# Banded attention on one core: the value's low half taken from a float32 copy by GpSimd, and three buffers of probability halves

## What is computed

```python
x = x + broadcast(v[:, 1:2]),  v = layernorm(x) @ W.T + b      # one row per sequence
x = x + ffn(layernorm(x))                                       # two mixes, sigmoid gate
# attention, 16 heads of 64, seen as rows of 1024-long sequences; banded, window 128
q, k = rope(proj(Wq, bq)), rope(proj(Wk, bk)); v = proj(Wv, bv)
scores = (q_block @ concat(k_previous_block, k_block).T) / 8, masked to kj in [qi, qi + 128]
ctx = softmax(scores) @ concat(v_previous_block, v_block)
x = x + ctx @ Wo.T + bo
x = x + ffn(layernorm(x))
```

## Time and profile before

| | |
|---|---|
| median of three runs | 1597.86 us |
| the profiled execution | 1600.48 us, its span 1598.6 us |
| busy over the span: TensorE, VectorE, ScalarE, GpSimd | 94%, 88%, 83%, 71% |
| TensorE granted clock, mean over the span | 0.985 |
| busy of 400 us in the middle of the attention: TensorE, VectorE, ScalarE, GpSimd | 382.25, 372.32, 338.95, 325.26 us |
| TensorE, line 1693 | 256 products with minus the identity |
| ScalarE, line 1530 | 128 copies of the low half |

### The profile page before, as it was taken

One profiled execution on the slowest core, in us unless ns is written; L12 is line 12 of the kernel. 1 busy time (PEld: TensorE's weight loads), 2 busy tenths in 40 slices (PEclk: granted clock), 3 DMA queues, 4 the chain that ended last, 5 costly groups with the idle time before them and its releaser, 6 DMA issues. The chain is left out here.

```text
span 1598.6 us, 46975 instructions
## 1 busy us (share of the span) xinstructions
PE 1497.0 (94%) x16866; PEld 1144.6 (72%) x16866; DVE 1403.0 (88%) x3860; ACT 1323.6 (83%) x2442; POOL 1134.8 (71%) x909
## 2 busy tenths in 40 slices
PE   5999978899999999999999999999999999889998
PEld 4888745577777677766767776766677777678887
DVE  6999669999999999999999999999999999857885
ACT  5999668888888888888888888888888878759996
POOL 4665367778787887877787878787887777623443
PEclk8999999999999999999999999999999999989999
DMA  5242248899999999999999999999999998962331
GB/s 214 93 126 93 90 80 140 166 173 174 181 176 175 170 172 174 182 172 179 171 173 172 168 180 178 177 173 179 168 168 169 177 162 159 174 162 85 107 107 67
DMA packets 729886, 247.94 MB, mean 155 GB/s; under 512 B 689588, under 2 KB 716472, under 8 KB 729656
## 3 DMA queue, kind: packets, MB, share of 16 engines
q1 hardware_dynamic: 711816, 228.93, 75.6%
q10 hardware_dynamic: 17840, 16.00, 3.7%
HBM read 47.73 MB, written 25.17 MB: 46 GB/s over the span
## 5 line engine op out<-in xcount | busy, mean ns | idle before, releaser
L1502 ACT ACTIVATE at_prob<-at_prob,at_top 128x256 f32<-128x256 f32 (+1 forms) x1024 | 428.3, 491 | 20.0 <-DVE at_top L1338 17.7
L1338 DVE CUSTOM_DVE_ANT_0 at_prob<-banks,at_masks,pre_s_scale 128x256 f32<-128x256 f32 (+1 forms) x1024 | 421.0, 471 | 26.5 <-PE banks L1778 10.1
L1350 DVE TENSOR_TENSOR at_halves<-at_prob,at_halves 128x1024 f16<-128x1024 f32 (+1 forms) x256 | 333.1, 1301 | 4.4 <-ACT at_halves L1511 4.3
L1663 PE MATMUL banks<-at_xt,pre_w_h 128*128 128x512 f16 x1024 | 298.2, 384 | 7.5 <-ACT at_v_l L1530 4.7
L1778 PE MATMUL banks<-at_kt,at_qt 32*128 32x256 f32 (+1 forms) x4096 | 252.4, 382 | 45.1 <-POOL at_qt L1240 20.5
L1778 PEld LDWEIGHTS banks<-at_kt,at_qt 32*128 32x128 f32 x4096 | 197.7, 186 | 106.7 <-issue 102.1
L1511 ACT ACTIVATE at_halves<-at_prob 128x1024 f16<-128x1024 f32 (+1 forms) x256 | 263.4, 1029 | 6.1
L1734 PE MATMUL banks<-at_v_h,at_pt 128*128 128x65 f16 x1984 | 208.7, 195 | 11.6 <-DMA at_pt<-at_halves 7.6
L1220 POOL TENSOR_TENSOR at_q_by<-at_q_first,at_tables 128x512 f32<-128x512 f32 x128 | 174.6, 1368 | 63.0 <-DVE at_halves L1350 61.0
L1230 POOL TENSOR_TENSOR at_kt<-at_k_by 128x512 f32<-128x512 f32 x128 | 171.7, 1341 | 64.6 <-DVE at_halves L1350 61.8
L1734 PEld LDWEIGHTS banks<-at_v_h,at_pt 128*128 128x128 f16 x1984 | 182.4, 98 | 46.3 <-issue 25.2
(11 more groups left out here) (124 smaller groups left out, 3311.8 us busy)
## 6 DMA issues: line engine op xcount, KB each, us to landing
f_x<-in_x SPq DMA_DIRECT2D x16, 512.0 KB, 3.6
x_after_ffn<-f_x SPq DMA_DIRECT2D x16, 512.0 KB, 2.6
f_x<-x_after_attention SPq DMA_DIRECT2D x16, 512.0 KB, 4.5
out_x<-f_x SPq DMA_DIRECT2D x16, 512.0 KB, 3.0
at_x_res<-x_after_ffn ACTq DMA_DIRECT2D x61, 128.0 KB, 2.8
x_after_attention<-at_x_res ACTq DMA_DIRECT2D x58, 128.0 KB, 1.9
at_x_ln<-x_after_ffn SPq DMA_DIRECT2D x32, 128.0 KB, 3.0
at_tables<-in_cos SPq DMA_DIRECT2D x16, 256.0 KB, 3.6
```

The costliest lines, as they stand in the source:

```text
L1338: last = nc.vector.tensor_tensor_reduce(out=prob[:, n % 2, h, low:2 * P], in0=s_ps[:, h, n % 2 * 2 * P + low:(n % 2 + 1) * 2 * P], in1=mas ...
L1350: nc.vector.tensor_tensor(parts[:, 1, :, :], prob[:, n % 2, :, keys_from(t, b):2 * P], parts[:, 0, :, :], ALU.subtract).then_inc(p_low, 1)
L1502: last = nc.scalar.activation(at, at, ACT.Exp, bias=top[:, n % 2, h:h + 1], scale=-1.0)
L1663: last = nc.tensor.matmul(pr_ps[:, half, :].rearrange("p (b t) -> p b t", b=SB), w[wp][:, k, at:at + P], xt[:, r, :, xp, k, :], start=n == ...
```

## The change

The product with minus the identity goes. ScalarE makes two copies of the projected values: the high half as before, and a whole float32 copy into a new SBUF buffer `v_full`, in the place where the low half was copied. GpSimd subtracts the high half from it and writes the low half. `v_full` takes the place in memory of the fourth buffer of `halves`, so `HB` is 3. On ScalarE, from step 5 on, both whole copies stand ahead of `exponentials(t, 3)` instead of behind it. `keys_of` waits for the whole copy instead of the low half. On GpSimd `v_low_of(t, 0)` stands between the key products and the wait for `p_low` of block 0, and `v_low_of(t + 1, 1)` at the end of the step. The constants lose the making of `neg_eye`.

```diff
-    HB = 4
+    HB = 3
+    v_full = sb("v_full", [P, 2, 2 * GROUP * HD])
 # gpsimd
+        def v_low_of(t, half):
+            if step(t):
+                pool.wait_ge(v_copied[half], t + 1)
+                if t < 2:
+                    pool.wait_ge(past.act_made, 2 * past.CHUNKS)
+                at = pair_of(t, half)
+                nc.gpsimd.tensor_tensor(v_l[:, at, :, :],
+                                        v_full[:, half, :].rearrange("p (b h d) -> p b h d", b=2, d=HD),
+                                        v_h[:, at, :, 0:HD], ALU.subtract).then_inc(v_low[half], 1)
             key_product(t + 1, 0)
             key_product(t + 1, 3)
+            v_low_of(t, 0)
             after_p_low(t, 0)
...
             bias_rows(t - 4)
+            v_low_of(t + 1, 1)
 # scalar
-                need(pt_in[n % 2], turned(n - HB))
+                need(pt_in[(n - HB) % 2], turned(n - HB))
-        def v_low_of(t, half):
-            if step(t):
-                act.wait_ge(v_rest[half], t + 1)
...
-                nc.scalar.activation(v_l[:, pair_of(t, half), :, :],
-                                     pr_ps[:, half, :].rearrange("p (b h d) -> p b h d", b=2, d=HD),
-                                     ACT.Copy).then_inc(v_low[half], 1)
+        def v_copy(t, half):
+            if step(t):
+                act.wait_ge(v_done[half], t + 1)
+                need(v_low[half], t)
+                if t == 0:
+                    act.wait_ge(past.gated_made, 2 * past.CHUNKS)
+                nc.scalar.activation(v_full[:, half, :], pr_ps[:, half, :], ACT.Copy).then_inc(v_copied[half], 1)
...
                 v_high_of(t + 1, 1)
                 v_high_of(t + 1, 0)
+                v_copy(t + 1, 1)
+                v_copy(t + 1, 0)
                 exponentials(t, 3)
-                v_low_of(t + 1, 1)
-                v_low_of(t + 1, 0)
 # tensor
-                need(v_low[half], t)
+                need(v_copied[half], t)
                 project(r, KC + t % NG * 2 * P, half, k_done[half])
...
             output(t - 5)
-            values_rest(t + 1, 1)
-            values_rest(t + 1, 0)
             values_product(t, 0)
```

More of the change, by code:

```diff
@@ L67 @@
                       "VALUED valued mix_made low_made r_done relu_made act_made gated_made x_made")
-AttentionStage = namedtuple("AttentionStage", "sync gpsimd vector scalar tensor STEPS XT_ALL PT_ALL v_done v_low stored "
+AttentionStage = namedtuple("AttentionStage", "sync gpsimd vector scalar tensor STEPS XT_ALL PT_ALL v_done v_copied stored "
                             "xt_in q_roped s_done p_low pt_in top_made ctx_made x_made RB")
@@ L79 @@
              "q_by": F + 40960, "k_first": F + 49184, "q_first": F + 51232, "bv_wide": F + 49184, "x_res": F + 53280,
-             "kt": F + 57376, "prob": F + 69664, "v_h": F + 77856, "v_l": F + 84096, "halves": F + 90240,
-             "pt": F + 106624, "c_halves": F + 114816, "tables": D, "masks": D + 8192, "neg_eye": D + 9216,
+             "kt": F + 57376, "prob": F + 69664, "v_h": F + 77856, "v_l": F + 84096, "halves": F + 90240, "v_full": F + 102528,
+             "pt": F + 106624, "c_halves": F + 114816, "tables": D, "masks": D + 8192,
              "out_bias": D + 10240}
@@ L678, in transposes @@
                 if past is not None and c == 0:
-                    pe.wait_ge(past.v_low[0], past.STEPS)
+                    pe.wait_ge(past.v_copied[0], past.STEPS)
                 pe.wait_ge(xn_made, 2 * (c + 1))
@@ L937, in attention_stage @@
     masks = sb("masks", [P, 2 * P])
-    neg_eye = sb("neg_eye", [P, P], F16)
     tables = sb("tables", [P, 2, 2, SB * P])
@@ L1002, in attention_stage @@
     v_high = [sem("v_first_high"), sem("v_second_high")]
-    v_rest = [sem("v_first_rest"), sem("v_second_rest")]
+    v_copied = [sem("v_first_copied"), sem("v_second_copied")]
     v_low = [sem("v_first_low"), sem("v_second_low")]
@@ L1018, in attention_stage @@
     x_made = sem("x_made")
-    EYE_MADE, MADE = 6, 7
+    MADE = 5
     LOADED = {-8: (4, 5), -7: (6,), -6: (7,), -5: (), -4: (), -3: (8, 9, 10)}
@@ L1291, in opening @@
                 nc.gpsimd.affine_select(out=part, in_=part, **rule).then_inc(made, 1)
[L1292 to L1295, removed]
         def first_std():
@@ L1522, in v_high_of @@
                                      ACT.Copy).then_inc(v_high[half], 1)
-        def v_low_of(t, half):
+        def v_copy(t, half):
             if step(t):
-                act.wait_ge(v_rest[half], t + 1)
-                if t < 2:
-                    act.wait_ge(past.act_made, 2 * past.CHUNKS)
-                nc.scalar.activation(v_l[:, pair_of(t, half), :, :],
-                                     pr_ps[:, half, :].rearrange("p (b h d) -> p b h d", b=2, d=HD),
-                                     ACT.Copy).then_inc(v_low[half], 1)
+                act.wait_ge(v_done[half], t + 1)
[3 more added lines that the diff above has]
+                nc.scalar.activation(v_full[:, half, :], pr_ps[:, half, :], ACT.Copy).then_inc(v_copied[half], 1)
         def carry_keys(t):
@@ L1682, in values @@
                                 w[wp][:, k, VC + g * 2 * P:VC + (g + 1) * 2 * P],
-                                start=blk == 0 and n == 0 and k == 0, stop=False, skip_group_check=True)
+                                start=blk == 0 and n == 0 and k == 0, stop=blk == 1 and n == 2 and k == CK - 1,
+                                skip_group_check=True)
                 last.then_inc(v_done[half], 1)
-        def values_rest(t, half):
-            if step(t):
[L1689 to L1697, removed]
         def keys_of(t, half):
@@ L1816, in attention_stage @@
     return AttentionStage(sync=sync, gpsimd=gpsimd, vector=vector, scalar=scalar, tensor=tensor, STEPS=STEPS,
-                 XT_ALL=xt_ready(NS - 1), PT_ALL=turned(4 * STEPS - 1), v_done=v_done, v_low=v_low, stored=stored,
+                 XT_ALL=xt_ready(NS - 1), PT_ALL=turned(4 * STEPS - 1), v_done=v_done, v_copied=v_copied, stored=stored,
                  xt_in=xt_in, q_roped=q_roped, s_done=s_done, p_low=p_low, pt_in=pt_in, top_made=top_made,
```

## The result

The changed kernel takes 1669.39 us, the median of four runs (1668.78 to 1672.37), against 1598.58 us (1597.71 to 1599.58, four runs) before. The ratio is 1.0447, with a 95% interval of 1.0434 to 1.046: 71 us slower. The forecast was 1682, in a range of 1612 to 1726.

The account below looks back on a forecast made before the run. A closed 18.40 us loop of scores, VectorE and GpSimd bounds the kernel, TensorE outside it. Mean step 19.9 against 18.59: 1.33 us over 63 steps, 84 us, on 1600.5 us, less 2.6, gives 1682 us; range 1612 to 1726.

Parts of the forecast that it names:

- The loop: Scores 2.11 us, VectorE to the end of block 1's `p_low_of` 10.27, GpSimd 6.02: together 18.40 us, the step's length.
- the rival with 1570 us: TensorE sets the pace and GpSimd's gaps take the new work: 28 us less; chance 0.08.
- half held: GpSimd's subtractions only partly overlap `p_low_of`; step grows 0.2 to 0.8 us, giving 1610 to 1650 us; chance 0.08.
- The sum: GpSimd's work plus exclusions per step, corrected to a mean of 19.9 us against 18.59, adding 84 us.
- 19.63: GpSimd's new step without rest, in us: 13.39 present work, 2.24 for two subtractions, 4.00 for four exclusions.
- 0.15: Us per step added for GpSimd reaching the wait for block 1 some 0.1 to 1 us early.
- 0.30: Us added to the mean step for the `inverse_std` of one step in four on GpSimd.
- 0.13: Us taken off the mean step for 16 narrow blocks that exclude GpSimd half as long.
- 0.08: Us taken off the mean step because the last eight steps have no `x_low_of` (0.67 us).
- 18.59: Mean step of the kernel before, in us, from (1386.5 - 214.0 - 1.2)/63.
- VectorE pays as well: `p_low_of` waits for GpSimd instructions, adding 0.3 to 0.7 us a step: 1700 to 1727 us; kept inside the forecast's 0.78.
- the budget: GpSimd's step before: 13.39 us work plus four exclusions at 1.00, 17.39 of 18.40 us, leaving 1.0 us free.

Follow-up runs that it names:

- the stand-in: Each kernel with DMA transposes replaced by plain DMAs and the reciprocal by a product with a constant: kernel before 1594.26 us, changed kernel 1668.86 us.

## Why the prediction was right, step by step

**The loop and TensorE.** The step that line 1693 is worth nothing held: the run without it saves nothing, and its time reappears as a wait for ScalarE. With it fell the rival with 1570 us.

**The excluded time.** The step "each `p_low_of` costs GpSimd 1.0 us, as a wait or as a hold" held, also for the float16 subtraction, which the rows of before could not show: 1.11 us free, 2.10 in the median. By the Trainium skill's rule ("SBUF — State Buffer", section on its two separate sides) that was to be expected, and the trace agrees. The page names no element type; that its rule covers float16 was my reading, and this run is what shows it. One reading beside it was wrong: the key products of the earlier trace rows (799.50 to 802.01) run mostly under products of VectorE that read PSUM (line 1420), not under `tops`, whose last begins at 799.45; under `tops` runs `context_low`, with its usual 2.14 us. The rival "half held" fell with the mean step, which grew by 1.15 us and not by 0.2 to 0.8; its own sum did not come out either, as 1.0 to 2.0 us saved of a growth of 1.4 leaves 0.4 at most.

**The sum.** This is the term that was too large, by its size and by a slip. The slip: 19.63 and 0.15, plus 0.30, less 0.13 and 0.08, is 19.87 us, and less 18.59 that is 1.28 us or 81 us; the 1.33 us and 84 us of the forecast don't follow from their own terms, by 3 us. The size: the mean step is (1456.8 - 211.8 - 1.2)/63 = 19.74 us against these 19.87, so it grew by 1.15 us, which is 72 us over 63 steps. The step shown has 19.57 us, where I had 19.8. Of these 0.2 us, 0.10 are the two subtractions, put in at 1.12 us each, which cost 1.07 from start to start (2.07 between 810.92 and 812.99, less the hold of 1.00); 0.04 are `bias_rows`, 0.68 from start to start and not 0.72; and 0.04 are the key products, which now run straight into a subtraction. Holds and the wait are 4.13 us (0.99, 1.00, 0.98 and 1.16), where I had 4.15 with the 0.15 that I added; that addition was drawn from a hand-made layout, and the run without waits shows it to be of the right size (0.19 us a step).

**The ends.** That the first query starts 2.2 us earlier (211.8 against 214.0) was not in my sum, and is a gain of as much. These errors all made the forecast too long, and the order on ScalarE, below, is one more of that sign; none was hidden by another.

**ScalarE.** I counted 0 for the order and the longer copy. In the stand-in the order is a gain of 6.5 us, which I had not seen: I looked for what the later exponentials delay, not for what the earlier copies release. The float32 copies take a median of 0.606 us, 0.03 more than the float16 ones had (0.578).

**Three buffers.** Counted 0, found 0 in the stand-in, and at most 1.9 us of added idle time on ScalarE in the changed kernel.

**VectorE pays as well.** This mechanism is there: a mean of 1597 ns for the `p_low_of` against 1301, and 55 of the 256 take over 2 us, where 7 did before. It runs beside GpSimd's chain and adds nothing to its budget beyond the small wait. The 1700 us and more of that case did not come.

**What stays open.** That both subtractions behind the queries would have cost the same was not tried; the budget says so, and no run does. Nor is it shown which property of a VectorE instruction makes it hold GpSimd, or how much the two subtractions would cost if nothing were held: no run takes the exclusion away and leaves the durations as they are.

## What to carry to other kernels

Before work goes to an engine with idle time, ask of each idle stretch whether an instruction could have run in it: a wait that lies under another engine's instruction is no free time if the two exclude each other, and the sign of that is in the durations of instructions that do overlap (1.27 us free, 2.27 held). Add up work and exclusions against the length of a step; here 17.4 of 18.4 us were taken in a step that showed GpSimd busy for 14.4. And an engine that is busy 94% of the span can be off the loop: look whether its next instruction starts when another engine's row ends.

## What the runs showed of the hardware

- A two-operand GpSimd instruction in SBUF (product, sum or subtraction) and a VectorE subtraction of two SBUF operands exclude each other, in both directions: 128x512 in float32 takes 1.27 or 2.27 us on GpSimd, 128x1024 takes 1.21 to 2.37 us on VectorE, by who comes first.
- Unexpected: a VectorE copy from float32 to float16 with one input holds GpSimd too, by about 0.5 us for its 0.68.
- The VectorE subtraction with one operand in PSUM took 0.68 us for 128x512, the GpSimd one 1.11 us free.
- Replacing transposes that filled the DMA engines by plain DMAs, with the DMA share cut to less than half, changed the time by 0.3% at most.
